# Attention and experts on one core: the value layer's second half moved into the next image's compressed tiles, and scores as four products over 32 partitions into four banks

## The reference

```python
q_c, k_c, v_c = project(x)                      # 4 heads of 32 channels
fk = unfold(k_c, 4, stride 2); fv = unfold(v_c, 4, stride 2)   # 225 blocks of 16 pixels
k_cmp = gelu((fk + pos) @ k_w1 + k_b1) @ k_w2 + k_b2           # 2048 -> 256 -> 128
v_cmp = gelu(fv @ v_w1 + v_b1) @ v_w2 + v_b2
attn_cmp = softmax(q_c @ k_cmp.T * SCALE)                      # 1024 x 225, per head
imp = attn_cmp.sum(heads).mean(pixels); idx = top_k(imp, 16)
attn_slc = softmax(q_s @ gathered_k.T * SCALE)                 # 1024 x 256, per head
g = sigmoid(gelu(x @ gate_w1 + gate_b1) @ gate_w2 + gate_b2)   # three gates per pixel
out = g0 * attn_cmp @ v_cmp @ P + g1 * attn_slc @ v @ P' + g2 * window_attention
```

## Time and profile before

| what | value |
|---|---|
| median of 3 runs | 748.17 us (747.45 to 748.37) |
| the profiled execution: its own time | 749.96 us |
| its span | 748.2 us, 16869 instructions |
| PE busy | 662.0 us, 88% of the span |
| DVE busy | 439.9 us, 59% |
| ACT busy | 443.2 us, 59% |
| mean granted clock of PE | 0.952 of 2.4 GHz |
| chain that ended last | PE 62%, DVE 16%, ACT 9% |

### The profile page before, as it was taken

How to read it: one execution, slowest core, us unless ns; L and a number is a source line. 1 busy time by engine, 2 the same in 40 slices (tenths; PEclk the granted TensorE clock), 3 DMA queues, 4 the chain that set the end, 5 groups by cost and what they waited for, 6 DMA issues and landing times.

```text
span 748.2 us, 16869 instructions
## 1 busy us (share of the span) xinstructions
PE 662.0 (88%) x5318; PEld 496.9 (66%) x5318; DVE 439.9 (59%) x1429; ACT 443.2 (59%) x1287; POOL 233.8 (31%) x341
## 2 busy tenths in 40 slices
PE   2997899999899999989999999877899998989992
PEld 1694467666557766555776656554468897989981
DVE  4206847553986754488676548777646653455443
ACT  1307844664883366487336648633767896878961
POOL 3200014200202473110247310042605477644551
PEclk9999999999999999989999998985899999999995
DMA  7301000000000010000001090001301334363215
GB/s 293 126 0 30 1 1 6 2 0 29 29 2 2 4 35 25 29 1 1 3 4 37 24 264 18 1 5 48 77 8 38 132 86 103 84 200 93 73 47 179
DMA packets 36353, 40.03 MB, mean 54 GB/s; under 512 B 12176, under 2 KB 27936, under 8 KB 35980
## 3 DMA queue, kind: packets, MB, share of 16 engines
q1 hardware_dynamic: 30412, 27.47, 12.8%
q0 software_dynamic: 4704, 9.40, 3.8%
q10 hardware_dynamic: 1152, 2.10, 0.8%
HBM read 25.64 MB, written 15.17 MB: 55 GB/s over the span
## 4 chain that ended last, share of the span: by engine, by line
PE 62%; DVE 16%; ACT 9%; issue 5%; DMA 3%; SPq 2%; POOL 2%; DVEq 1%; ACTq 0%; POOLq 0%
PE ps L1713 8%; PE ps L1788 8%; PE ps L1830 6%; PE ps L1773 6%; PE ps L2173 6%; PE ps L1718 5%; PE ps L2191 5%; PE ps L1860 3%; ACT r_P L927 3%; DVE nmx L1241 2%; PE ps L1890 2%; PE ps L1933 2%; PE ps L1875 2%; PE ps L1902 1%; DVE r_P L1251 1%
## 5 line engine op out<-in xcount | busy, mean ns | idle before, releaser
L927 ACT ACTIVATE r_P<-ps,nmx 128x225 f32<-128x225 f32 (+1 forms) x192 | 86.0, 468 | 62.6 <-DVE nmx L1241 62.6
L1241 DVE TENSOR_REDUCE nmx<-ps 128x4 f32<-128x900 f32 (+1 forms) x64 | 73.7, 1156 | 24.7 <-PE ps L1830 24.1
L778 POOL DMA_INDIRECT xs_d<-pay,pos x64 | 62.4, 974 | 35.9 <-DVE nmx L1241 20.8
L800 POOL DMA_INDIRECT z_d<-xhatT,xrow_room x54 | 52.7, 977 | 61.9 <-DVE xhatT L1632 55.2
L702 POOL TENSOR_TENSOR rstd<-vpe,minus_half 128x8 f32<-128x8 f32 x8 | 13.6, 1701 | 187.0 <-DVE vpe L1178 187.0
L1713 PE MATMUL ps<-ident,r_P 128*128 128x128 f32 (+1 forms) x384 | 54.6, 284 | 13.0 <-DVE R L1263 7.7
L1713 PEld LDWEIGHTS ps<-ident,r_P 128*128 128x128 f32 (+1 forms) x384 | 45.7, 152 | 26.7 <-issue 9.8
L1620 DVE TENSOR_TENSOR hv<-ps,x_sb 128x128 f32<-128x128 f32 x78 | 22.7, 291 | 67.8 <-PE ps L2191 51.4
L752 POOL TENSOR_TENSOR r_gh<-r_gh,nmw 113x392 f32<-113x392 f32 (+1 forms) x20 | 15.6, 781 | 140.5 <-DVE nmw L1280 140.3
L1788 PEld LDWEIGHTS ps<-r_vc,w_sb 128*128 128x128 f32 x256 | 46.1, 188 | 19.4 <-issue 15.9
L1788 PE MATMUL ps<-r_vc,w_sb 128*128 128x225 f32 x256 | 58.8, 375 | 0.0
(11 more groups left out here) (242 smaller groups left out, 1461.6 us busy)
## 6 DMA issues: line engine op xcount, KB each, us to landing
xrow_room<-xs_d SPq DMA_DIRECT2D x54, 65.0 KB, 2.0
x_sb<-x SPq DMA_DIRECT2D x4, 512.0 KB, 3.5
w_sb<-w1k SPq DMA_DIRECT2D x1, 2048.0 KB, 7.6
w_sb<-w1v SPq DMA_DIRECT2D x1, 2048.0 KB, 12.1
...
w_sb<-fw SPq DMA_DIRECT2D x4, 512.0 KB, 10.0
...
```

The costliest lines, as they stand in the source:

```text
L778: gp.indirect_dma_start(xs_d, bass.IndirectOffsetOnAxis(pos[:, NT * k + t:NT * k + t + 1], 0), pay[:, k, t, :], None).then_inc(scattered, 16)
L800: gp.indirect_dma_start(z_d, bass.IndirectOffsetOnAxis(xrow(n)[:, C + 1:C + 2].bitcast(U32), 0), yrow(n), None).then_inc(y_out[n % XRING], 16)
L927: last = sc.activation(Pb[t % NRING][:, h, 0:m], bank(name)[:, (h % 2) * m:(h % 2) * m + m], ACT.Exp, bias=nmx[:, t % NRING, h:h + 1], acc ...
L1241: ve.tensor_reduce(nmx[:, t % NRING, :].rearrange("p (a h) -> p a h", a=2), v.rearrange("p a (h m) -> p a h m", h=2), AX.X, ALU.max, negat ...
```

## The change

Two edits are made together.

The scores of a tile become four products over 32 partitions, one per head, each into a bank of its own. `kbd` holds the keys once, without zeros. Every tile now takes banks 0 to 3, all four claimed ahead of the first product; DVE takes the maxima in two instructions of two banks each, and ACT waits for each pair.

The value layer's second half (16 products, `mw`) of image b leaves the selected tiles of image b - 1 (and the opening) for steps 0 to 3 of image b's own compressed tiles, four products a step. `mw` holds bank 6 for those steps, so the extras of steps 0 to 3 all pass through bank 7. Its Gelu stands on ACT in step 4, ahead of the `qs` copies. The gate logits (`gg`) and the compressed values (`gv`) become separate tiles, in steps 0 and 5. Within a step of the compressed tiles PE makes the scores of tile t + 1 after the extras of step t; some extras move a step or two (`gc` from 4 to 6, `qs` from 5 to 4, `qw` later).

```diff
 def psum_plan():
     def scores(s, t, b):
-        for k in range(2):
-            put(2 * (t % 2) + k, f"S{s}{t}{'ab'[k]}@{b}")
+        for i in range(HEADS):
+            put(i, f"S{s}{t}{i}@{b}")
...
+        put(6, f"mw@{b}")
         for t in range(NT + F_LAG):
+            if t == 0:
+                extra = around((7,))
+            if t == MW_SLOTS:
+                extra = around((7, 6))
...
 def compressed_extras(b, t):
-    late_head = {0: ("gv", "kw0"), 1: ("kw1",), 4: ("kw2",)}
-    own = {1: ("vw0",), 4: ("gc0", "gc1"), 5: ("qs0", "qs1", "qw0"), 6: ("qw1",), 7: ("vw1", "qw2"),
-           8: ("gb",), 10: ("vw2", "vw3", "gw0", "gw1")}
+    late_head = {0: ("kw0",), 1: ("kw1",), 4: ("kw2",)}
+    own = {1: ("vw0",), 4: ("qs0", "qs1"), 5: ("gv", "qw0"), 6: ("gc0", "gc1"), 7: ("vw1", "qw1"),
+           8: ("gb", "qw2"), 10: ("vw2", "vw3", "gw0", "gw1")}
...
 # ACT, compressed_tiles
                     if t == 4:
                         if prev >= 0:
                             window_keys(b, 2)
-                        gates_by_channels(b, "gc", g_cmp)
-                    if t == 5:
+                        hidden_values(b, 1)
                         for i in range(2):
                             queries(f"qs{i}@{b}", qTs, i, 1)
...
 # DVE
             def maxima(b, s, t, m):
-                dve.wait_ge(*filled(f"S{s}{t}a@{b}"))
-                dve.wait_ge(*filled(f"S{s}{t}b@{b}"))
-                v = two_banks(f"S{s}{t}a@{b}")[:, :, 0:2 * m]
-                ve.tensor_reduce(nmx[:, t % NRING, :].rearrange("p (a h) -> p a h", a=2),
-                                 v.rearrange("p a (h m) -> p a h m", h=2), AX.X, ALU.max, negate=True)\
-                  .then_inc(max_ready, 1)
+                for i in range(0, HEADS, 2):
+                    dve.wait_ge(*filled(f"S{s}{t}{i}@{b}"))
+                    dve.wait_ge(*filled(f"S{s}{t}{i + 1}@{b}"))
+                    ve.tensor_reduce(nmx[:, t % NRING, i:i + 2], two_banks(f"S{s}{t}{i}@{b}")[:, :, 0:m],
+                                     AX.X, ALU.max, negate=True).then_inc(max_ready, 1)
...
             def selected_keys(b):
                 flip(b, 0, "bk_s")
-                for h in range(HEADS):
-                    p0, p1 = HD * h, HD * h + HD
-                    last = ve.scalar_tensor_tensor(
-                        out=kbd[p0:p1, h % 2, :].rearrange("p (k i) -> p k i", i=NPOS), in0=kflip[p0:p1, :, 1, :],
-                        scalar=col("m1", p0, p1), in1=khalf[p0:p1, :, :], op0=ALU.mult, op1=ALU.add)
-                last.then_inc(kbd_sel_ready, 1)
+                ve.scalar_tensor_tensor(
+                    out=kbd[:, :].rearrange("p (k i) -> p k i", i=NPOS), in0=kflip[:, :, 1, :],
+                    scalar=col("m1"), in1=khalf[:, :, :], op0=ALU.mult, op1=ALU.add).then_inc(kbd_sel_ready, 1)
...
 # PE
             def scores(b, s, t, m):
                 q = qT if s == "c" else qTs
-                for k in range(2):
-                    name = f"S{s}{t}{'ab'[k]}@{b}"
-                    claim(name)
-                    p0 = 64 * k
-                    mm(bank(name)[:, 0:2 * m], q[p0:p0 + 64, 128 * t:128 * t + 128],
-                       kbd[p0:p0 + 64, :, 0:m], start=True, stop=True).then_inc(full_sem(name), 1)
+                for h in range(HEADS):
+                    claim(f"S{s}{t}{h}@{b}")
+                pe.nop(nofuse=True)
+                for h in range(HEADS):
+                    name, p0 = f"S{s}{t}{h}@{b}", HD * h
+                    mm(bank(name)[:, 0:m], q[p0:p0 + HD, 128 * t:128 * t + 128], kbd[p0:p0 + HD, 0:m],
+                       start=True, stop=True).then_inc(full_sem(name), 1)
...
             def compressed_tiles(b):
                     if 0 <= t - T_LAG < NT:
                         turned_probabilities(b, "c", t - T_LAG, (M0, M1))
-                    if t + 1 < NT:
-                        scores(b, "c", t + 1, NB)
...
+                    if t == 3:
+                        for i in range(2):
+                            if h < B:
+                                image_by_tokens(h, i)
+                            value_part(b, t, i)
...
                         gates_by_channels(b, "gw", 2)
+                    if t + 1 < NT:
+                        scores(b, "c", t + 1, NB)
...
 # PE, selected_tiles
+                    if t < NT and h < B:
+                        value_layer(h, range(2 * t, 2 * t + 2))
                     if t + 1 < NT:
                         scores(b, "s", t + 1, 256)
-                    if t < NT and h < B:
-                        value_layer(h, range(4 * t, 4 * t + 4))
```

175 lines of the change are left out of this document (97 added, 78 removed).

## The result

The change makes the kernel slower, and by more than was forecast:

| what | before | after |
|---|---|---|
| median | 748.27 us (747.45 to 750.17, 4 runs) | 813.79 us (813.12 to 815.42, 4 runs) |
| span of the profiled execution | 748.2 us | 812.3 us |
| PE busy | 662.0 us, 88% | 657.9 us, 81% |
| granted clock, mean | 0.952 | 0.90 |

What follows compares the result with a forecast made beforehand. PE bounds the selected tiles; PE, DVE and ACT are nearly full in the compressed ones. From 748.2 us, -4.9 (image 0), +18.8 (images 1 and 2), +13.1 (image 3) and +8 (clock) gave 783, own range 770 to 798, overall 758 to 812.

Steps and rivals of the forecast that it cites:

- Part 1: Scores' products on PE: about 0.6 us a tile, saving 0.33 to 0.46 a tile, some 25 us in all.
- Part 2, the ring: Selected tiles: with one set of banks, scores wait for the last exponential; a step takes 3.45 us, seven take 24.2.
- The tail: Behind the last selected tile PE has less left to do: 2.7 us gained.
- the POOL wait: Window stage: selected keys in one operation bring PE's wait of 1.22 us for POOL forward by about 1.2.
- Part 3: Compressed tiles of images 1 and 2: copies and extras lengthen the steps, 45.2 us against 31.8; +12.7 after small returns.
- steps 0 and 4: Image 1's compressed tiles: step 0 waits for gate logits, 4.5 us; step 4 for router's logits and Gelu, 10.0.
- Part 4: Images 0 and 3: -1.6 us and +10.8; with the selected tiles' share, -4.9 and +13.1.
- Part 5, the clock: PE's granted clock falls to about 0.80 in the long steps; the part on the path 2 us an image, +8.
- Rival C: PE stays at 1.2 GHz through compressed and selected tiles; a selected step becomes 4.3 us; 811 us in all; 15%.
- Rivals A: PE's sum decides, its extras filling the waits for scores: 718 us, or 733 for half of it; 7%.
- B: Compressed steps 2, 3, 4 and 6 overlap better than summed, 7 us less in three images: 762 us; 18%.
- D: The four score products do not overlap: 1.2 us a tile more in 64 tiles, 860 us; 4%.

Runs made afterwards that it cites:

- a_warm: Changed kernel with unread products ahead of turned tiles and value products drawn to the first steps in the selected tiles; 808.6 us, 1.0763 to the kernel before.
- one set: Kernel before with only the scores' edit: four products over 32 partitions into banks 0 to 3, scores ahead of the extras; 825.5 us, ratio 1.1005.

## Why the prediction was wrong

- **What bounds the kernel, and the mechanism.** Right in the main. The scores' head start over ACT and DVE was what kept three engines full, and the change took it away. The releasers named for `kw0`, `kw2` and `qs`, the longest step, the ring in the selected tiles and the 0.45 to 1.06 for a tile of scores (0.71) are in the trace.
- **Part 1.** Right: 0.4 us a tile saved on PE. Over the execution the scores took 82.4 us of PE and take 54.6, 28 less where some 25 was forecast. PE's busy time fell only from 662.0 to 657.9, since others run longer at the lower clock (the value layer's products 58.8 before, 67.8 now), and what was saved turned into waiting.
- **Part 2, the ring.** Mis-sized: 3.45 forecast, 3.73 measured. The terms given for a selected tile (0.68, 1.93, 0.6, 0.15) add to 3.36, not 3.45, so by them 0.37 is missing: 0.26 between the reading of the last sum (done at 154.77) and the scores (155.03), for which no term stood, 0.05 at the maxima and 0.06 from the scores to the next maxima. Against 3.45 it is 8 us over 28 selected steps. The tail was nearly right (-2.5 against -2.7), the POOL wait only in part, since 0.82 of it came back as the wait of the first scores for four banks.
- **Part 3.** Right in the pattern, 45.2 forecast against 50.9 in image 1. 4.7 of the 5.7 are in steps 0 and 4, and their rows put most of it down to products at 1.2 GHz: 1.5 in step 0, and in step 4 `kw2` +0.5, the queries +1.8, the scores +0.5. Table loads as priced, 20 in all where there were 12. Two steps were rounded up (their terms add to 4.4 and 9.8, not 4.5 and 10.0). What lies behind the last maxima was too hopeful: 1.9 less an image was forecast up to the first selected maxima, and images 1 and 2 have 0.3 and 1.1 less.
- **Part 4.** Image 0's steps were forecast at 33.9 in sum and are 36.6. How -1.6 for image 0 and +10.8 for image 3 come out of the steps is not shown in the forecast, so these two can't be taken apart.
- **Part 5, the clock: the step that failed.** It took 2 us an image, 8 in all, as what of the clock lies on the path; its own ends, 0 and 7 an image, were wide enough. As an estimate from the rows at either level, it was 4.3 in each of images 1 to 3 (1.5 in step 0, 2.8 in step 4), 1.5 in the first three selected steps of images 0 to 2 (4.24 against 3.73), and 3.6 in image 3, where all seven are 4.25: about 21 us against 8. a_warm confirms the selected steps of images 0 to 2 and step 0 of image 1; in image 1's step 4 the queries take 3.76 or 3.78 in every run with the scores behind the extras and the layer moved, so what step 4 would be with them at 2.4 GHz was not run. The error was the sentence "Most of that lies in waits". The low stretches are longer than the waits (212.4 to 225.9 covers both waits of step 4 and all products between and behind them), and these products are what everybody waits for. A sign was in the forecast's own row: the scores that took 1.87 do not follow the wait of 1.70 but come 3.05 us behind its end, with the router's logits at full clock between.
- **Rival C** was nearer in time (811) and right that a selected step of 4.3 would come, but not in its extent: it asked for the low clock through both stages, and in the profiled execution it is there in 16 of 28 selected steps and in stretches of the compressed ones. TensorE: Matmul & The Clock Gate, in the Trainium skill (A second HAM failure mode), describes a clock that goes back and forth between its two levels as PE idles between bursts. The trace agrees in kind, with granted clocks of 1.00 and 0.50 in turn; but in step 4 the clock fell behind 3.6 us in which PE was busy 3.51.
- **Rivals A, B and D** are refuted: PE is busy 34.84 of 50.85 us in image 1's compressed tiles, steps 2, 3, 4 and 6 there are all longer than their sums, and the four products run together (0.71).

Ring 8 and clock 13 make 21 of the 30 us missed. The rest is spread: steps 1, 2, 3 and 6 of the compressed tiles are 0.1 to 0.5 longer than forecast, the opening is 0.8 longer, and there is the wait of the first scores. No run took these apart.

The forecast's parts hold only for all three edits together, since each was priced with the others in place. Asked for *one set* alone, the same theory gave 765 to 780 and the chip 825; so the sum near the right size is in part luck, and was no proof of the theory behind it.
